# Cross-attention loop of a Perceiver block: softmax and context split reordered, four transposition banks, value products per head on 32-column positions

## The reference, cut to what matters

```python
qh = (q @ Wq + bq).reshape(b, n, H, HD)            # b = 8, n = 64, H = 16, HD = 32
kh = (k @ Wk + bk).reshape(b, k.shape[1], H, HD)   # k = v = ctx_1024, 512 rows
vh = (v @ Wv + bv).reshape(b, v.shape[1], H, HD)
scores = jnp.einsum('blhe,bshe->bhls', qh, kh)
attn = jax.nn.softmax(scale * scores, axis=-1)
out = jnp.einsum('bhls,bshd->blhd', attn, vh)
return out.reshape(b, n, H * HD) @ Wo + bo
```

## Time and profile before

| | us |
|---|---|
| median of three runs | 737.51 |
| the profiled execution's own time | 737.64 |
| its span, first to last instruction | 735.9 |
| loop steps, period of one step (of seven) | 33.6 |

### The profile page before, as it was taken

The page is one execution under the profiler, slowest core; times in us unless marked ns, Lnnn a source line. Parts: engine busy times, 40 slices in busy tenths (PEclk is TensorE's granted clock), DMA queues, the critical chain, the costliest instruction groups (busy, mean ns, idle before and its releaser), DMA issues.

```text
span 735.9 us, 9457 instructions
## 1 busy us (share of the span) xinstructions
PE 685.9 (93%) x3760; PEld 440.2 (60%) x3760; DVE 302.4 (41%) x619; ACT 239.7 (33%) x468; POOL 42.5 (6%) x43
## 2 busy tenths in 40 slices
PE   6699999999999999869998989999999999999996
PEld 5468687877768687447897565344444444444532
DVE  4844726445362717576678654111111111111112
ACT  4444434354443525144675122111111111111110
POOL 0800000000000000065000010000000000000000
PEclk9999999999999999989999999999999999999999
DMA  8110101011033000030209740799999999999921
GB/s 302 55 58 1 58 2 57 1 58 55 4 136 151 1 1 1 1 100 24 102 16 419 280 201 1 264 348 376 407 366 412 355 405 356 384 377 380 391 81 60
DMA packets 14344, 129.63 MB, mean 176 GB/s; under 512 B 2720, under 2 KB 2848, under 8 KB 6240
## 3 DMA queue, kind: packets, MB, share of 16 engines
q1 hardware_dynamic: 12384, 127.09, 44.7%
q10 hardware_dynamic: 1920, 1.97, 0.9%
HBM read 126.03 MB, written 1.05 MB: 173 GB/s over the span
## 4 chain that ended last, share of the span: by engine, by line
PE 77%; DVE 13%; ACT 4%; issue 3%; DMA 1%; SPq 1%; ACTq 1%; DVEq 0%
PE ps L964 17%; PE ps L1206 14%; PE ps L1238 8%; PE ps L1213 7%; PE ps L1047 4%; PE ps L1245 4%; PE ps L1127 4%; PE ps L1037 4%; DVE ctx_lo L680 2%; PE ps L1227 2%; PE ps L1164 2%; PE ps L1073 2%; PE ps L1010 1%; PE ps L1176 1%; DVE neg_max L727 1%
## 5 line engine op out<-in xcount | busy, mean ns | idle before, releaser
L860 DVE TENSOR_TENSOR hid<-hid,ps 128x256 f32<-128x256 f32 (+1 forms) x32 | 17.6, 553 | 141.6 <-PE ps L1206 91.8
L702 DVE COPY probs_T<-ps 128x512 f32<-128x512 f32 x32 | 22.1, 692 | 99.9 <-PE ps L1037 99.9
L476 ACT ACTIVATE probs<-ps,neg_max 128x512 f32<-128x512 f32 x64 | 43.8, 687 | 57.1 <-DVE neg_max L727 57.1
L585 ACT ACTIVATE hid<-ps 128x256 f32<-128x256 f32 (+1 forms) x32 | 15.7, 490 | 141.6 <-PE ps L1213 86.5
L1238 PE MATMUL ps<-w_d,hid_T 128*64 128x512 f32 x256 | 58.4, 598 | 1.4 <-ACT hid_T L600 1.4
L1206 PE MATMUL ps<-w_u,x_slot 128*64 128x512 f32 x256 | 58.4, 598 | 0.0
L1206 PE MATMUL ps<-w_g,x_slot 128*64 128x512 f32 x256 | 57.8, 593 | 0.0
L964 PE MATMUL ps<-wv_hi,ctx_hi 128*128 128x512 f32 x128 | 52.5, 410 | 4.1 <-POOL wv_lo L395 4.1
L964 PE MATMUL ps<-wv_lo,ctx_hi 128*128 128x512 f32 x128 | 50.5, 395 | 0.0
L964 PE MATMUL ps<-wv_hi,ctx_lo 128*128 128x512 f32 x128 | 50.5, 394 | 0.0
L964 PE MATMUL ps<-ctx_hi,wk_hi 128*128 128x512 f32 x112 | 44.5, 398 | 0.0
(11 more groups left out here) (192 smaller groups left out, 1167.9 us busy)
## 6 DMA issues: line engine op xcount, KB each, us to landing
w_u<-in_wu SPq DMA_DIRECT2D x16, 2048.0 KB, 16.2
w_d<-in_wd SPq DMA_DIRECT2D x16, 2048.0 KB, 14.7
w_g<-in_wg SPq DMA_DIRECT2D x16, 2048.0 KB, 10.4
ctx_raw<-in_ctx SPq DMA_DIRECT2D x7, 1024.0 KB, 4.8
w_qkv<-in_wqkv SPq DMA_DIRECT2D x1, 3072.0 KB, 13.8
ws_g<-in_wsg SPq DMA_DIRECT2D x1, 2048.0 KB, 7.8
ws_u<-in_wsu SPq DMA_DIRECT2D x1, 2048.0 KB, 7.6
ws_d<-in_wsd SPq DMA_DIRECT2D x1, 2048.0 KB, 22.4
```

The lines of the kernel that those rows point to most:

```text
L476: act.activation(probs[:, p, :], bank(SCORE[p]), ACT.Exp, bias=neg_max[:, p:p + 1], scale=1.0, accum_out=row_sum[:, p:p + 1]).then_inc(exp ...
L702: dve.tensor_copy(probs_T[:, ht % 2, 1].rearrange("p s c -> p (s c)"), bank(TRANS[1])).then_inc(pT_done[1], 1)
```

## The change: what it does

- The TRANS banks become four: 2, 3 for even head tiles, 5, 6 for odd ones. T0 and T1 both stand between key tiles 2 and 3; then come A0, A1, T2, T3, A2, A3. T2 and T3 wait for the copies of T0 and T1.
- attend works per head: 32 columns of v_s as weights against that head's 64 columns of probs_T, to the output partitions 32j to 32j+31 and 64 columns. Four matmuls per context tile instead of two, on four positions of 32 columns.
- o_out becomes one instruction over 128 partitions with 256 elements each.
- ctx_high and ctx_low of batch b+1 move from the middle of the step (ahead of the exponentials, of the maxima) to its start.
- softmax takes the four maxima of a group first and the four normalisations after them.

```diff
-        PROJ, TRANS, AV = (0, 1), (2, 3), 4
-        SCORE = (5, 6, 7, TRANS[0], 5, 6, 7, TRANS[1])
+        PROJ, TRANS, AV = (0, 1), ((2, 3), (5, 6)), 4
+        SCORE = (5, 6, 7, 2, 5, 6, 7, 3)
@@ ACT @@
             def probs_T_out(b, tiles=range(KT)):
                 for ht in tiles:
                     act.wait_ge(pT_ps, b * PAIRS + 2 * ht + 1)
-                    act.copy(probs_T[:, ht % 2, 0]..., bank(TRANS[0])).then_inc(pT_done[0], 1)
+                    act.copy(probs_T[:, ht % 2, 0]..., bank(TRANS[ht % 2][0])).then_inc(pT_done[0], 1)
             def step(b, par, more=True):
+                if more:
+                    ctx_high(b + 1, 1 - par)
                 k_out(b, 0)
                 k_out(b, 1)
                 k_out(b, 2)
-                probs_T_out(b - 1, (0,))
+                probs_T_out(b - 1, (0, 1))
                 k_out(b, 3)
-                probs_T_out(b - 1, (1, 2, 3))
-                if more:
-                    ctx_high(b + 1, 1 - par)
+                probs_T_out(b - 1, (2, 3))
                 values_and_exponents(b)
@@ DVE (probs_T_out as on ACT, with TRANS[ht % 2][1]) @@
             def o_out(b):
                 dve.wait_ge(o_ps, b * KT + KT)
-                for hh in range(HPT):
-                    rows = slice(HD * hh, HD * (hh + 1))
-                    blocks = slice(1, 3) if hh % 2 else slice(0, 4, 3)
-                    dve.tensor_tensor(o_T[rows, :, bass.ds(b * L, L)]..., bank(AV)...[rows, :, blocks, :],
-                                      bias_v[rows, :]..., ALU.add).then_inc(o_done, 1)
+                dve.tensor_tensor(o_T[:, :, bass.ds(b * L, L)],
+                                  bank(AV)[:, 0:KT * L].rearrange("p (t l) -> p t l", l=L),
+                                  bias_v[:].unsqueeze(2).to_broadcast([P, KT, L]), ALU.add).then_inc(o_done, 1)
             def softmax(b):
...
                         dve.tensor_reduce(neg_max[:, p:p + 1], bank(SCORE[p]), AX.X, ALU.max,
                                           negate=True).then_inc(max_done, 1)
-                        if i:
-                            normalise(b, p - 1)
-                    normalise(b, GROUP * g + GROUP - 1)
+                    for i in range(GROUP):
+                        normalise(b, GROUP * g + i)
             def step(b, par, more=True):
+                if more:
+                    ctx_low(b + 1, 1 - par)
                 probs_T_out(b - 1)
                 o_out(b - 1)
-                if more:
-                    ctx_low(b + 1, 1 - par)
                 softmax(b)
@@ PE @@
             def probs_transpose(b, ht):
...
-                    if ht:
-                        pe.wait_ge(pT_done[pr], b * KT + ht)
+                    if ht >= 2:
+                        pe.wait_ge(pT_done[pr], b * KT + ht - 1)
                     for st in range(NS):
-                        ins = pe.transpose(ps[:, TRANS[pr], P * st:P * (st + 1)],
+                        ins = pe.transpose(ps[:, TRANS[ht % 2][pr], P * st:P * (st + 1)],
                                            probs[:, 2 * ht + pr, P * st:P * (st + 1)], ident[:])
             def attend(b, ht):
...
                 for st in range(NS):
-                    for pr in range(2):
-                        cols = slice(2 * HD * (2 * ht + pr), 2 * HD * (2 * ht + pr + 1))
-                        ins = pe.matmul(ps[64 * pr:64 * (pr + 1), AV, P * ht:P * (ht + 1)], v_s[:, st, cols],
-                                        probs_T[:, ht % 2, pr, st, :], start=(st == 0), stop=(st == NS - 1),
-                                        skip_group_check=True)
+                    for j in range(HPT):
+                        pr, side = j // 2, (j + ht) % 2
+                        cols = slice(P * ht + HD * j, P * ht + HD * (j + 1))
+                        ins = pe.matmul(ps[HD * j:HD * (j + 1), AV, L * ht:L * (ht + 1)], v_s[:, st, cols],
+                                        probs_T[:, ht % 2, pr, st, L * side:L * (side + 1)],
+                                        start=(st == 0), stop=(st == NS - 1), skip_group_check=True)
                 ins.then_inc(o_ps, 1)
             def attention(b):
                 pe.wait_ge(v_done, b * NS + NS)
-                for ht in range(1, KT):
-                    probs_transpose(b, ht)
-                    attend(b, ht - 1)
-                attend(b, KT - 1)
+                attend(b, 0)
+                attend(b, 1)
+                probs_transpose(b, 2)
+                probs_transpose(b, 3)
+                attend(b, 2)
+                attend(b, 3)
             def step(b, par):
                 project_k(b, par, range(KT - 1))
                 probs_transpose(b - 1, 0)
+                probs_transpose(b - 1, 1)
                 project_k(b, par, (KT - 1,))
                 attention(b - 1)
                 values_and_scores(b, par)
...
             probs_transpose(B - 1, 0)
+            probs_transpose(B - 1, 1)
             attention(B - 1)
-            pe.wait_ge(o_done, B * HPT)
+            pe.wait_ge(o_done, B)
```

More of the change, by code:

```diff
@@ L468, in probs_T_out @@
                     act.wait_ge(pT_ps, b * PAIRS + 2 * ht + 1)
-                    act.copy(probs_T[:, ht % 2, 0].rearrange("p s c -> p (s c)"), bank(TRANS[0])).then_inc(pT_done[0], 1)
+                    act.copy(probs_T[:, ht % 2, 0].rearrange("p s c -> p (s c)"), bank(TRANS[ht % 2][0])).then_inc(pT_done[0], 1)
             def values_and_exponents(b, early=0):
@@ L701, in probs_T_out @@
                     dve.wait_ge(pT_ps, b * PAIRS + 2 * ht + 2)
-                    dve.tensor_copy(probs_T[:, ht % 2, 1].rearrange("p s c -> p (s c)"), bank(TRANS[1])).then_inc(pT_done[1], 1)
+                    dve.tensor_copy(probs_T[:, ht % 2, 1].rearrange("p s c -> p (s c)"), bank(TRANS[ht % 2][1])).then_inc(pT_done[1], 1)
             def o_out(b):
                 dve.wait_ge(o_ps, b * KT + KT)
-                for hh in range(HPT):
-                    rows = slice(HD * hh, HD * (hh + 1))
-                    blocks = slice(1, 3) if hh % 2 else slice(0, 4, 3)
[L710 to L713, removed]
+                dve.tensor_tensor(o_T[:, :, bass.ds(b * L, L)],
+                                  bank(AV)[:, 0:KT * L].rearrange("p (t l) -> p t l", l=L),
+                                  bias_v[:].unsqueeze(2).to_broadcast([P, KT, L]), ALU.add).then_inc(o_done, 1)
             def normalise(b, p):
```

## The result

| | before | after |
|---|---|---|
| median of the runs on the same chip, us | 738.59 | 714.83 |
| profiled execution, its own time, us | 737.64 | 715.17 |
| its span, us | 735.9 | 713.4 |
| period of a middle step, us | 33.60 | 30.55 |

The ratio is 0.9681, with a 95% interval of 0.9656 to 0.9705: 3.2% faster. The forecast was 716.1 us, with a step of 30.6.

A forecast was written before the change was run, and what follows sets the result against it. PE, busy for 93% of the span, was taken to bound the kernel, so gains come from its work or stalls. 8.5 + 12.4 + 1.4 - 0.8 = 21.5 us off 737.64 gives 716.1 us, range 713.5 to 719.

The forecast's parts named there:

- Part 1: PE's wait for an exponential ahead of score group 1: 1.42 us in six steps goes, 8.5 us saved.
- Part 2: Context split at the start of the step: covered, except key tile 2 of step 1 starts 0.8 us later, once.
- Part 3: Transpositions and value products on PE: 5.48 us a step instead of 7.03, 1.55 saved eight times, 12.4 us.
- X: Bare time of one new value product in attend, 16 matmuls: taken as 0.45 us, bounds 0.44 and 1.75.
- Part 4: o_out at the end, ahead of the residual product: one instruction, 1.4 us saved; inside the loop it is hidden.
- C: Rival in attend: positions of 32 columns don't run side by side, X = 1.75, 754 us; chance 0.06.
- B: Rival in the value products: half-sized rounds don't get shorter, X = 0.87, 726.2 us; chance 0.16.
- D: Rival: the stall moves on to waits for k_out or value copies, Part 3 holds, 724.6 us; chance 0.09.

The follow-up runs named there:

- e5: Kernel before with only ctx_high and ctx_low moved to the start of the step: 731.47 us, ratio 0.9905.
- e1: Changed kernel with ctx_high and ctx_low put back to the middle of the step: 714.31 us, ratio 0.9669.
- e6: Kernel before with only the narrow value products and the one-instruction o_out: 718.06 us, ratio 0.9714.
- e8: Kernel before with only the four maxima of a group ahead of its four normalisations: 733.76 us, ratio 0.9922.
- e7: Kernel before with only the four transposition banks and the new order of PE and ACT, wide products kept: 735.04 us, ratio 0.9942.
- e4: Changed kernel with all four heads of a tile writing output partitions 0 to 31, one position: 754.32 us, one run.
- e3: Changed kernel with the normalisations put back between the maxima: 718.15 us, ratio 0.9717.

## Why the prediction was right, point by point

- **Part 1, the stall (8.5 us).** Size right, cause too narrow. S1 no longer waits, and e5 shows that the move of the context split alone does it. But e1 shows that the change doesn't need it: three edits attack the same 1.42 us (the move, the shorter o_out, the order of the maxima), and I gave it to the first. The sentence "ctx_low is gone from this place" should have been followed by the same sum with ctx_low still there. Alone, e5 takes the whole of it, e6 takes the whole of it as well, and e8 takes 0.83 a step. So the parts alone bring 7.9 + 21.3 + 4.3 + 5.6 = 39 us in the medians, and together 24. By the loop's length it is 7.0 + 20.7 + 3.1 + 5.2 = 36.0 us against 22.5, and the stall accounts for nearly all of the difference of 13.5: 8.5 in e5, 8.5 in e6 and 4.8 in e8 make 21.8, of which 8.5 can be had, 13.3 less.
- **Part 2, the cost in step 1 (0.8 us).** Key tile 2 starts at 61.67 instead of 61.17: 0.5. Four exponentials ended a little earlier (the cast starts at 59.11, not 59.35). No k_out is late in later steps.
- **Part 3, 1.55 us a step.** Right in the whole and nearly so in each term: X is 0.44 where I took 0.45, T3 to A3 1.91 where I took 1.94, and T2 to T3 0.93 where I took 1.02, since the kind changes on one side only. T1 adds 0.87 between the key tiles (T0 and T1 take 1.66 up to the next key tile, T0 alone took 0.79). With the 4.46 from 160.75 to 165.21 the part from T1 to S0 is 5.33 where I had 5.48. Without the S1 stall the step got 33.60 - 1.42 - 30.55 = 1.63 us shorter.
- **The reading of the earlier trace rows was wrong in one place, and the sum was spared by luck.** I read T2 to T3, 2.04 us, as the time of the copy. It was PE's own work (1.02 + 1.02) that filled it; DVE's copy had ended 0.22 us before T3 started, and only T3's second four transpositions need it. A3 needs both copies from its start, so there the wait is real: 1.07 to the start of the copy, 0.69 for the copy and 0.15 to A3 make 1.91. That this lies in the middle of the 1.82 to 2.04 that I had read off is the luck. In e6, where this reading decides, it made me forecast 12.9 us instead of 21.3. It also means that the four banks are worth little: 0.27 us a step on top of e6, 0.31 alone (e7).
- **Part 4, o_out (1.4 us).** 1.83 from its start to the residual product became 0.47.
- **The sum.** By the starts in the profile: step 1 -2.57 (1.42 + 1.63 - 0.5), the five further steps with the stall -15.26, the last -1.62, behind the last S1 -3.05. Together -22.5, forecast -21.5.
- **The rivals.** e4 measures C's world at 754.32 (forecast 754) and shows why it isn't ours. B needs X = 0.87, and 0.44 was measured. D didn't come: S0 to S1 is 6.7 us, and PE waited once for a key tile. The trace has 64 records in 1.03 us, 16 ns each, over four positions. The Trainium skill's floor of about 25 ns from start to start ("TensorE: Matmul & The Clock Gate", "Wait — 56ns, not 53.3ns?") doesn't hold across positions, and the measurement decides; within one position no run here went below 55 ns. This counts records, as the prediction did. Each fp32 matmul of the program is two of them; counted by matmuls it is 32 ns here, and only the bursts lie below the floor, as the eight records that start within 0.07 us in the earlier trace rows.

## What to carry to other kernels

When several edits shorten one stall, work out each of them with the others present, and alone; the stall can be won only once. Matmuls with few output columns gain by what they don't stream: half of what the wide products wrote was thrown away, and the narrow ones, four positions side by side, took half the time (X 0.44 us instead of 0.87). When a row seems to show a latency, ask whether the engine had other work for just that long, and which half of a buffer the first instruction behind it needs.

## What the hardware showed besides

The median of e3 lies 2 us above what its loop explains. Behind the loop the code is the same in both kernels. Here are two stages of it, each counted from the start of the residual product, in the changed kernel and then in e3 (length, busy us by engine, clock):

```profile
277.64:317.64 40.00, 32.98 (x110) 21.06 (x111) 27.59 (x53) 15.26 (x30) 16.18 (x11) 0.91 0.15 47
397.64:427.64 30.00, 24.67 (x112) 18.06 (x111) 18.68 (x66) 6.05 (x12) 2.38 (x3) 0.94 0.38 162
```

```profile
279.20:319.20 40.00, 32.99 (x108) 21.01 (x109) 27.57 (x52) 14.71 (x29) 15.63 (x11) 0.87 0.16 47
399.20:429.20 30.00, 24.88 (x108) 18.19 (x107) 18.91 (x67) 5.27 (x10) 2.38 (x3) 0.89 0.40 170
```

The granted clock is 0.91 and 0.94 of full speed in the one, 0.87 and 0.89 in the other. By the trace the clock is at its lower level (1.2 GHz) for 6.8 and 3.4 us in the changed kernel and for 10.2 and 6.8 us in e3. Set side by side, the starts of the same instructions drift apart by 0.5 us in the first stage and by 0.85 in the second, and by at most 0.03 elsewhere: that is the 1.4 us. In both kernels the first stretch at the lower level begins while PE idles for 5.1 us (up to 298.06 in the changed kernel); why it is longer in e3 no run here shows. The pattern repeats. The ten profiles with 10.2 us at the lower level behind the loop took 435.2 to 436.0 us there, the four with more (e3, e6, e7, e8) 436.7 to 437.2. Ahead of the loop S1 of batch 0 starts anywhere from 53.6 to 55.7 us among these runs, and that isn't explained by the clock alone. So two kernels with equal loops can differ by 2 us; the period of a step is free of it.

A change between kinds of matmul (128 to 32 or 64 weight columns, or from transposing to multiplying) costs 0.15 us here, which shows where groups are small: eight transpositions take 1.02 us between products instead of 0.87, and a product group of e6 0.59 instead of 0.44. Between a key tile and a transposition it is nearly nothing: in the kernel before, T0 and the key tile behind it take 3.65 us from start to next start, against 0.87 and 12 x 0.227 = 2.72 bare.
